# One attention and mixture-of-experts block on one core: the opening in a new order, one group's denominators summed on VectorE, one weight quarter staged elsewhere

## What is computed

```python
def _L0_xcond_ref(q, k, v, k_length):
    s = SCALE * jnp.log(k_length.astype(jnp.float32))[:, None, None, None]
    attn = jnp.einsum('bhdq,bhdk->bhqk', qh, kh)
    attn = jax.nn.softmax(s * attn, axis=-1)
    out = jnp.einsum('bhqk,bhdk->bhdq', attn, vh)
...
sh = gelu(xt @ sw1 + sb1) @ sw2 + sb2
sh = sh + gelu(xt @ swd) @ swu
out = out + 0.2 * sh
...
x = x + _L0_xcond_ref(_layernorm(x, axis=-1), ctx_2048, ctx_2048, itok_B_779_1933)
x = x + _L0_ffn_ref(_layernorm(x, axis=-1), L0_ffn_gate_w, ...)
```

## Time and profile before

| | |
|---|---|
| median of three runs | 1346.81 us |
| profiled execution | 1353.0 us |
| its span, first to last instruction | 1351.2 us |
| PE busy | 1305.0 us (97%) |
| DVE, ACT, POOL busy | 839.0, 704.5, 250.8 us |
| mean granted TensorE clock | 0.991 |
| first down-projection matmul | 104.83 us after the start |

### The profile page before, as it was taken

How to read it: one execution, slowest core, us unless ns; L and a number is a source line. 1 busy time by engine, 2 the same in 40 slices (tenths; PEclk the granted TensorE clock), 3 DMA queues, 4 the chain that set the end, 5 groups by cost and what they waited for, 6 DMA issues and landing times.

```text
span 1351.2 us, 26893 instructions
## 1 busy us (share of the span) xinstructions
PE 1305.0 (97%) x11055; PEld 950.2 (70%) x11072; DVE 839.0 (62%) x1408; ACT 704.5 (52%) x1056; POOL 250.8 (19%) x219
## 2 busy tenths in 40 slices
PE   5788999999999999999999999999999999999997
PEld 2143646556464737375788889999999988888895
DVE  7777768778778787765552844728456284472730
ACT  4757675757676666673332533535344353442521
POOL 4540000000001041433200311203012030120012
PEclk9899999999999999999999999999999999999999
DMA  9514141222356223324826757767576675767413
GB/s 273 183 55 125 33 110 48 83 67 71 79 72 70 84 67 102 98 52 72 266 94 134 196 141 188 170 141 197 145 201 147 139 198 142 186 145 152 95 25 40
DMA packets 182572, 165.08 MB, mean 122 GB/s; under 512 B 104889, under 2 KB 125513, under 8 KB 182450
## 3 DMA queue, kind: packets, MB, share of 16 engines
q1 hardware_dynamic: 170162, 138.15, 39.0%
q0 software_dynamic: 12288, 25.21, 10.9%
HBM read 109.47 MB, written 34.15 MB: 106 GB/s over the span
## 4 chain that ended last, share of the span: by engine, by line
PE 86%; DVE 4%; ACT 4%; issue 3%; POOL 1%; DMA 0%; POOLq 0%; ACTq 0%; DVEq 0%
PE banks L1821 25%; PE banks L1851 24%; PE banks L1755 11%; PE banks L1737 10%; PE banks L1677 4%; PE banks L1657 4%; PE banks L1625 3%; DVE rowmax L1281 2%; ACT hidden L1058 1%; ACT QS L1045 1%; PE banks L1711 1%; PE banks L1686 1%; PE banks L1862 1%; PE banks L1723 1%; POOL w1l L942 1%
## 5 line engine op out<-in xcount | busy, mean ns | idle before, releaser
L1851 PE MATMUL banks<-hidden,w2h 128*128 128x0 bf16 x2048 | 306.1, 269 | 0.0
L1058 ACT ACTIVATE hidden<-banks,scales 128x512 f32<-128x512 f32 x256 | 171.1, 686 | 101.5 <-PE banks L1657 86.4
L1851 PEld LDWEIGHTS banks<-hidden,w2h 128*128 128x128 bf16 x2048 | 198.6, 98 | 20.5
L1281 DVE TENSOR_REDUCE rowmax<-banks 128x1 f32<-128x512 f32 x256 | 172.5, 684 | 40.3 <-PE banks L1625 38.3
L1851 PE MATMUL banks<-hidden,w2l 128*128 128x0 bf16 x1024 | 192.3, 269 | 0.0
L1432 DVE TENSOR_TENSOR w1l<-stage,w1h 128x2048 bf16<-128x2048 f32 x32 | 73.2, 2291 | 186.3 <-ACT w1h L1135 186.3
L1755 PE MATMUL banks<-w2h,hidden 128*128 128x512 bf16 x512 | 184.3, 379 | 0.0
L1152 ACT ACTIVATE hf<-banks,b1cols 128x640 f32<-128x640 f32 x128 | 101.1, 790 | 123.1 <-PE banks L1821 107.7
L1163 ACT ACTIVATE yT<-banks 128x640 uint16<-128x640 uint16 x56 | 36.3, 701 | 215.3 <-PE banks L1851 215.3
L1821 PE MATMUL banks<-eth,w1h 128*128 128x0 bf16 x1024 | 133.0, 273 | 0.0
L1821 PE MATMUL banks<-eth,w1l 128*128 128x0 bf16 x1024 | 132.9, 273 | 0.0
...
...
## 6 DMA issues: line engine op xcount, KB each, us to landing
...
QS<-split_parts SPq DMA_DIRECT2D x48, 128.0 KB, 2.7
KS<-split_parts SPq DMA_DIRECT2D x48, 128.0 KB, 3.1
...
```

Source lines behind the costliest of these rows:

```text
L1058: ac.activation(prob[n % NPH], bank(score_bank[unit]), ACT.Exp, scale=scales[:, g // 2:g // 2 + 1]).then_inc(s_exp, 1)
L1281: dv.reduce_max(rowmax[g % 2][:, i:i + 1], bank(score_bank[unit]), X_AXIS).then_inc(s_max, 1)
L1851: issued = mm(bank(b0 + j)[:, skips[j]:CAP].shape_from_register(used_cols(e, j)), w[:, fb, rows], of_choice(a[:, fb, :], j, skips[j]).shap ...
```

## The change

Three things are changed, all in window 0.

1. The list of the opening is written anew. `first_scores`, `first_exponentials` and `second_exponentials` take the place of the code for window 0. Group 0's first two scores go ahead of the preparation of group 1; the second weight quarter is loaded after both groups' parts are read back; four scores of group 1 go ahead of `rows` of group 0, and after that one score goes with each exponential; quarters are split beside exponentials 3, 7 and 11 of group 0 and 1, 4, 8 and 11 of group 1; ten scores of group 2 are made beside group 1's exponentials instead of eight (`AHEAD`). `average` of group 0 and the GpSimd instruction of its second normalisation stand ahead of the low parts of all w2 quarters.
2. Group 0 joins `SUMMED`: its four rounds of ones matmuls become six additions on VectorE and one round. Groups 1 and 3 stay as they are.
3. Quarter 7 is staged in one tensor that now holds `lowf` and the three `yout` buffers, so `late_stage` is free for the sums. `rank` of pass 1 waits for all low parts; the wait of the first sum for them goes. The first use of banks 6 and 7 by the shared network waits for the last score or exponential of the opening that was in that bank, not for all of group 1.

```diff
@@ -45,10 +45,11 @@
-SUMMED = [2, *range(4, GROUPS)]
+SUMMED = [0, 2, *range(4, GROUPS)]
+AHEAD = 10
...
         def next_scores():
-            for _ in scores((a + 2) * UNITS + EARLY, (a + 3) * UNITS):
+            for _ in scores((a + 2) * UNITS + (EARLY if w else AHEAD), (a + 3) * UNITS):
...
-    pieces, left_over, fourth = [], [], [prepare(3)]
-    QUARTERS = (4, 8, 13, 18, 23, 28)
-
-    def split_quarter(n):
-        add("w_split", n)
-        pieces.extend((n, a) for a in range(4))
-
-    def low_piece():
-        if pieces:
-            add("w_lo", *pieces.pop(0))
...
+    left_over, pieces = [], [(n, a) for n in range(8) for a in range(4)]
+    def low_pieces(count=1):
+        for _ in range(count):
+            if pieces:
+                add("w_lo", *pieces.pop(0))
+    def half_step(g, n):
+        t, k = divmod(n, GH)
+        if t < QT and k in ((1,) if g in SUMMED else (0, 1)):
+            add("values", g, t, k)
+    def units(g, *names):
+        for name in names:
+            add(name, g)
+    def first_scores():
+        for g in range(2):
+            add("load", g)
+            add("c_load", g)
+        for g in range(2, 4):
+            add("load", g)
+        add("small")
+        add("w_load", 0)
+        units(0, "stats", "aggr", "rstd", "norm", "x_hi")
+        add("k_hi", 1)
+        add("turn_v", 0)
+        units(0, "x_lo", "c_lo", "store")
+        units(1, "stats", "aggr", "rstd")
+        score = scores(0, UNITS)
+        for i, _ in enumerate(score):
+            if i == 1:
+                units(1, "norm", "x_hi", "x_lo", "c_lo", "store")
+                units(0, "bounce")
+                units(1, "turn_v", "bounce")
+                for n in range(1, 4):
+                    add("w_load", n)
+                    if n > 1:
+                        add("c_load", n)
+                add("rank_load")
+                for n in range(4, 8):
+                    add("w_load", n)
+                add("fills", 0)
+                add("w_split", 0)
+            if i == 4:
+                add("scales")
+            if 2 < i < 7:
+                low_pieces()
+        add("parts", 0)
+    def first_exponentials():
+        score = scores(UNITS, 2 * UNITS)
+        for _ in range(4):
+            next(score)
+        for _ in max_rows(0):
+            pass
+        rows = max_rows(1)
+        for i in range(UNITS):
+            if i % 2 and i > GH:
+                sums.append((i, (0, i // GH, i % GH // 2)))
+            add("exp", 0, i)
+            next(score, None)
+            if i in (3, 7, 11):
+                add("w_split", 1 + i // GH)
+            elif i > 3:
+                low_pieces()
+            if i == 1:
+                units(2, "stats", "aggr", "rstd")
+            if i == 5:
+                add("norm", 2)
+            if i == 9:
+                add("x_hi", 2)
+            if i == 11:
+                units(2, "x_lo", "c_lo", "bounce")
+            if i == 12:
+                add("parts", 1)
+                units(3, "stats", "aggr", "rstd")
+            if i == 13:
+                next(rows)
+            if i > 13:
+                next(rows, None)
+                next(rows, None)
+            ready_sums(i - 1)
+            if i > 5:
+                half_step(0, i - 6)
+        for _ in rows:
+            pass
+    def second_exponentials():
+        score = scores(2 * UNITS, 3 * UNITS)
+        for i in range(UNITS):
+            add("exp", 1, i)
+            if i in (1, 4, 8, 11):
+                add("w_split", 4 + (1, 4, 8, 11).index(i))
+            elif i:
+                low_pieces(2 if i > 11 else 1)
+            ready_sums(UNITS + i - 1)
+            if i < 4:
+                half_step(0, i + 10)
+            if i == 3:
+                add("ones", 0)
+            if i == 0:
+                add("wd", E)
+                add("norm", 3)
+                add("b2_parts")
+            if i == 2:
+                add("x_hi", 3)
+            if i == 3:
+                for _ in average(0):
+                    pass
+                units(0, "stats2", "aggr2", "rstd2")
+                units(3, "x_lo", "c_lo", "bounce")
+            if i == 6:
+                add("norm2", 0)
+            if i >= UNITS - AHEAD:
+                next(score)
+            if i == 9:
+                add("turn", 0)
+            if i == 11:
+                units(0, "gate", "xt_lo", "logit")
+            if i > 5:
+                half_step(1, i - 6)
+        low_pieces(99)
+        add("fills", 1)
+    first_scores()
+    first_exponentials()
+    second_exponentials()
+        if w:
+            exponentials_and_down(w)
...
-        lowf = sb("lowf", [WIDE, SLOTS], F32)
-        yout = [sb(f"yout{i}", [P, D], F32) for i in range(3)]
+        lowf_yout = sb("lowf_yout", [P, SLOTS + 3 * D], F32)
+        lowf = lowf_yout[0:WIDE, 0:SLOTS]
+        yout = [lowf_yout[:, SLOTS + i * D:SLOTS + (i + 1) * D] for i in range(3)]
...
-        hstage += [xt_stage[:, :], *(hidden[:, k * FB * PASS:(k + 1) * FB * PASS].bitcast(F32) for k in range(2)), late_stage[:, :]]
+        hstage += [xt_stage[:, :], *(hidden[:, k * FB * PASS:(k + 1) * FB * PASS].bitcast(F32) for k in range(2)), lowf_yout[:, P:P + 2048]]
...
+                first = w == 0 or (unit[0] == "score" and g == 2 and i < AHEAD)
...
+                    if first:
+                        last_first[b] = unit
...
+                    if p == 1:
+                        act.wait_ge(s_wlog, 32)
...
-                        if g == SUMMED[0]:
-                            dve.wait_ge(s_wlog, 32)
-                        else:
+                        if g != SUMMED[0]:
...
                 if was is None:
-                    pe.wait_ge(s_exp, UNITS * (2 if b > 5 else GROUPS))
                     if b > 5:
-                        pe.wait_ge(s_max, 2 * UNITS + EARLY)
+                        was = last_first[b]
+                        pe.wait_ge(s_max if was[0] == "score" else s_exp, nth[was])
+                    else:
+                        pe.wait_ge(s_exp, UNITS * GROUPS)
```

86 lines of the change are left out of this document (12 added, 74 removed).

## The result

The changed kernel takes 1351.45 us, the median of 20 runs (1350.7 to 1352.91). The kernel before takes 1350.42 us over 20 runs on the same chip (1346.71 to 1352.43). The ratio is 1.0018, 95% interval 1.0012 to 1.0024: slower by about 2.4 us, less than the 0.3% that the prediction called no change. Forecast were 1342.7 us and a gain of 4.1. One run of a later series of the kernel before took 1935 us at a granted clock of 0.755, and the ratios leave it out.

A forecast was written before the change was run, and what follows sets the result against it. PE, busy 97% of the span, was taken as the bound outside the opening; there gains of 0 at A, 3.1 at B, 4.4 at C and 4.1 at D gave 1346.81 - 4.1 = 1342.7 us, range 1338.5 to 1348.5.

The forecast's parts named there:

- Mark A: First exponential of group 0: forecast at 28.5 us against 28.55 before, gain 0, bounds +1.5 and -1.5.
- Mark B: Start of group 1's exponentials: forecast at 50.8 us against 53.9 before, gain 3.1, bounds 1.5 and 5.5.
- the price of a sum: VectorE additions for group 0's denominators: 1.22 us each, plus half a GpSimd piece, 0.6 us in all, for two of three.
- Mark C: First gelu of the shared network: forecast at 76.1 us against 80.52 before, gain 4.4, waiting for quarter 6.
- x2t: ScalarE's copy of the turned x2, ahead of the table load: forecast near 65.5 us against 68.46 before.
- GpSimd's gate: Group 0's power stands ahead of all w2 pieces; 12 follow it, so quarter 6 ends at 76.0 and holds the first gelu.
- T: The power of group 0's second normalisation on GpSimd: forecast at 61.5 us against 65.30 before.
- Mark D: First down-projections, end of the opening: forecast at 100.4 us against 104.49 before, gain 4.1.
- Behind D: After the first down-projections PE never pauses, so D's gain is the span's; nothing moves by more than 0.5 us.
- Rival 1: GpSimd's gate does not decide; T at 58 or 59, C at 74, D at 98: gain 6.5, 1340.3 us; chance 0.25.
- Rival 2: Group 2's operands return late from DRAM, PE stands 5 us: gain 0 to 1, 1346.3 us; chance 0.17.
- Rival 3: Slower: sums and low-rank steps wait whole GpSimd pieces, delaying T and GpSimd's one queue: 1350.3 us; chance 0.11.

The follow-up runs named there:

- e1: The changed kernel with group 0's denominators from ones matmuls again, without its six sums; new order and staging kept: ratio 0.9980, 1348.24 us.
- e10: e1 with quarter 7 staged in `late_stage` as before and the first sum's wait for the low parts put back: ratio 0.9989, 1349.87 us.
- e11: e1 run again unchanged, in a later series: ratio 0.9984, 1349.08 us.
- e4: The changed kernel with the 12 low parts of weight quarters 1 to 3 replaced by GpSimd zero fills, which read nothing: ratio 0.9979, 1348.34 us.
- e5: e1 with the low parts of weight quarters 1 to 3 replaced by GpSimd zero fills: ratio 0.9980, 1348.67 us.
- e9: The changed kernel, sums kept, with the four b2 steps moved right behind group 0's MS: ratio 1.0004, 1352.21 us.
- e12: e9 with the casts and low parts of wd moved ahead of the last three sums: ratio 1.0008, 1352.85 us.

## Why the prediction was wrong

**Mark A, right**: forecast 28.5, came 28.16; group 1's operands 23.3, came 23.21.

**Mark B, right**: forecast 50.8, came 50.57. But the price of a sum in it was not: 1.22 us each and 0.6 us of waiting for two of three. They took 1.58, 2.09 and 2.09, 2.1 us over their work. The net cost was still near the forecast: without the sums B came at 49.63, 50.03 and 49.93 (e1, e10, e11), 0.5 to 0.9 us sooner, so slack took up the rest. Here the number was right and its term was not.

**Mark C, the step that failed**: "x2t near 65.5, behind which ScalarE reaches the table load at 73 to 74", and with it "Quarter 6 is done at 61.5 + 0.6 + 13.9 = 76.0 ... it is now what the first gelu waits for". The power came at 62.77 (1.3 late), x2t at 67.97 (2.5 late), the table load at 77.77 (4 late). Quarter 6 was done at 77.8, and the gelu waited for PE. The path was wrong: not GpSimd's gate but ScalarE's waits for PE decide C.

The terms were mis-sized one by one. The last sum ended at 50.87 for the forecast 50.7. From there to the power it took 1.2 us more than forecast: wd's steps 4.96 us for 3.9 (1.2 without GpSimd), and the denominators' chain 4.4 for 4.0. From the power to x2t it took 5.2 us for 4.0. From x2t to the table load it took 9.8 us for 7.5 to 8.5, although the prediction's own row of the kernel before has 77.71 - 68.46 = 9.25 there; the shorter one was given no reason. The same holds for ScalarE's list as a whole, priced at 21.4 us "with no wait" from group 1's start and at 22 to 23 with x2t in it: it took 27.2 with 19.27 busy. Its exponentials hang on PE, PE on the maxima of group 2, and these stand behind the whole chain of denominators on VectorE (the row of maxima at 65.14). So a late chain costs twice: at x2t, and at exponentials behind it.

Under these terms lies the one that made the change look good, the price of contention between VectorE and GpSimd. All six sums took 9.62 us for 7.3, wd's steps 3.8 us over their work, and GpSimd's 12 pieces 18.22 for 13.5. The prediction gave the six sums 0.6 us of waiting in all, and only on VectorE's side, although its own row showed GpSimd held up too (1.46 us for a power). It never asked what the new order would do without them: T comes at 58.2 to 58.6 then (e1, e10, e11), 4.1 to 4.5 us sooner, and the time falls by 3.9 to 5.1 us (e10, e11, e1). e4 against the changed kernel, and e5 against e1, show that this loss needs GpSimd's reads.

**Mark D**: C to D took 23.28 us where 24.3 was forecast, right within 1 us. **Behind D** the prediction had "Whatever D gains, the span gains, since behind it PE goes on without a pause worth naming", and "nothing should move by more than 0.5 us". Both were wrong. There is a pause: from 124 to 128 us PE was busy for 1.07 of 4 us in the kernel before, and the page's slices read 5, 7, 8, 8 and only then 9, nine tenths from the fifth slice and not from the fourth. And D to E took 39.55 in the execution shown and 41.76 in the changed one. In the fourteen other executions it took 40.1 to 42.3, so the execution shown was the odd one, and the 1.6 us gained at D against it were none.

**Rivals.** Rival 1 was right that GpSimd's gate does not decide, and wrong in the rest: the power was late, not early. Rival 2 (group 2's operands) did not come: the copy issued at 45.22 was read back from 48.16 on, and no score of group 2 waited for a DMA. Rival 3 had the sign and the cause: the sums and the low-rank steps waiting whole pieces. Its path was another, through ScalarE's waits and not through GpSimd's queue. It was given 0.11, and a waiting sum was priced at half a piece.

The Trainium skill (SBUF — State Buffer, section Who interferes with whom) says that a VectorE instruction with two SBUF inputs contends with a GpSimd instruction that reads SBUF, but not with one that only writes it. The trace agrees in both halves: sums took up to 2.1 us beside pieces, and 1.21 and 1.23 beside e4's fills. The row maxima, which read PSUM, kept 0.6 us throughout.

**The starting time**: 1346.81 us of three runs stands for 1350.42 of twenty; 3.6 us of the distance to the forecast 1342.7 is this.

Open: at E the changed kernel is 0.6 us late, by the ratio 2.4, with e9 and e12, which have nearly its marks, at 0.5 and 1.1 us. Part of it is in the samples: the profiled executions of the kernel before are slow ones of their kind, and that of the changed kernel ran 2 us quicker behind E than thirteen of the others (1204.5 us for 1206.3 to 1207.1), and why was not run down; nor why the three kernels' ratios differ.
